# AdaLN block with linear attention and a mixture of experts: the first superblock in another order, LayerNorm and gates in pieces

## The reference, cut to what matters

```python
mod = (silu(c) @ wmod).reshape(1, 6, 1, -1)           # sa, ca, ga, sb, cb, gb
ga = sign(ga) * max(|ga|, 0.25); gb = likewise
h = layernorm(x) * (1 + ca) + sa                      # x: 1 x 4096 x 256
q, k, v = split(h @ w_qkv)                            # 16 heads of 64
q = softmax(q * SCALE, over the 64); k = softmax(k, over the tokens)
x = x + ga * ((per head q (k^T v)) @ w_out + b_out)
h = layernorm(x) * (1 + cb) + sb
x = x + gb * moe(h)                                   # 8 experts, top 2, gelu MLP 256-1024-256
```

## Time and profile before

| | us |
|---|---|
| median of 3 runs | 918.45 (918.38 to 919.68) |
| time of the profiled execution | 919.26 |
| its span | 917.5 |
| TensorE busy | 825.5 (90%) |
| VectorE busy | 571.7 (62%) |
| ScalarE busy | 498.4 (54%) |
| GpSimd busy | 344.2 (38%) |
| mean granted clock of TensorE | 0.95 |

### The profile page before, as it was taken

One profiled execution on the slowest core, in us unless ns is written; L12 is line 12 of the kernel. 1 busy time (PEld: TensorE's weight loads), 2 busy tenths in 40 slices (PEclk: granted clock), 3 DMA queues, 4 the chain that ended last, 5 costly groups with the idle time before them and its releaser, 6 DMA issues.

```text
span 917.5 us, 17514 instructions
## 1 busy us (share of the span) xinstructions
PE 825.5 (90%) x5836; PEld 770.2 (84%) x5837; DVE 571.7 (62%) x1257; ACT 498.4 (54%) x978; POOL 344.2 (38%) x304
## 2 busy tenths in 40 slices
PE   4849789999999888995499999999999999999994
PEld 4738678888888776984399999999999999999994
DVE  4677777777777652579546565656647575665552
ACT  4325446555554441359566665757567575665552
POOL 1213133334333131300135455455545555454442
PEclk9979899999999998995589999999999999999998
DMA  8300000000000013243515252252533525232222
GB/s 293 105 0 1 1 1 1 1 1 1 1 1 1 1 46 104 93 138 118 186 30 139 42 138 46 41 135 44 138 46 61 122 42 137 42 47 46 46 42 29
DMA packets 45214, 57.52 MB, mean 63 GB/s; under 512 B 7794, under 2 KB 39220, under 8 KB 45044
## 3 DMA queue, kind: packets, MB, share of 16 engines
q0 software_dynamic: 14400, 20.24, 13.7%
q1 hardware_dynamic: 30772, 36.76, 12.0%
HBM read 38.24 MB, written 18.75 MB: 62 GB/s over the span
## 4 chain that ended last, share of the span: by engine, by line
PE 79%; DVE 9%; issue 4%; ACT 4%; DMA 2%; POOL 1%; SPq 0%; ACTq 0%; DVEq 0%; POOLq 0%
PE ps L1436 23%; PE ps L1424 22%; PE ps L1269 8%; PE ps L1230 8%; PE ps L1288 6%; PE ps L1338 3%; PE ps L1278 2%; PE ps L1407 2%; ACT at_lo L736 2%; DVE q_max L857 1%; DMA wmod_sb<-in_L_wmod 1%; PE ps L1358 1%; DVE ln_s L841 1%; DVE k_blk L917 1%; PE ps L1348 1%
## 5 line engine op out<-in xcount | busy, mean ns | idle before, releaser
L791 ACT ACTIVATE hid<-ps,b_col 128x256 f32<-128x256 f32 x296 | 122.3, 464 | 120.9 <-PE ps L1424 120.9
L1151 DVE TENSOR_TENSOR hid_lo<-hid,hid_hi 128x512 fp32r<-128x512 f32 x148 | 102.5, 692 | 113.2 <-ACT hid_hi L799 111.1
L1436 PE MATMUL ps<-w_hi,hid_hi 128*128 128x256 f32 x592 | 170.2, 287 | 1.6 <-DVE hid_lo L1151 1.6
L1424 PE MATMUL ps<-xT_hi,w_hi 128*128 128x256 f32 x592 | 168.5, 285 | 2.2 <-DVE xT_lo L1128 2.2
L1424 PE MATMUL ps<-xT_hi,w_lo 128*128 128x256 f32 x592 | 168.3, 284 | 0.0
L1424 PE MATMUL ps<-xT_lo,w_hi 128*128 128x256 f32 x592 | 168.2, 284 | 0.0
L1436 PE MATMUL ps<-w_hi,hid_lo 128*128 128x256 f32 x592 | 166.5, 281 | 0.0
L1436 PE MATMUL ps<-w_lo,hid_hi 128*128 128x256 f32 x592 | 166.4, 281 | 0.0
L580 POOL DMA_INDIRECT out<-y,y_id x74 | 133.9, 1810 | 52.3 <-DVE y L1160 37.9
L504 POOL TENSOR_TENSOR q_n<-q_exp,q_rec 128x1024 f32<-128x1024 f32 x32 | 61.0, 1906 | 212.6 <-DVE q_rec L865 212.6
L1424 PEld LDWEIGHTS ps<-xT_hi,w_hi 128*128 128x128 f32 x592 | 113.8, 192 | 2.6 <-issue 2.6
(11 more groups left out here) (194 smaller groups left out, 1513.1 us busy)
## 6 DMA issues: line engine op xcount, KB each, us to landing
w_raw<-in_L_ffn_W SPq DMA_DIRECT2D x16, 1024.0 KB, 6.9
x_all<-in_L_attn_x SPq DMA_DIRECT2D x8, 512.0 KB, 10.3
out<-x_all SPq DMA_DIRECT2D x8, 512.0 KB, 3.0
xrows<-x_all SPq DMA_DIRECT2D x8, 512.0 KB, 3.0
wqk_raw<-in_L_attn_w_qkv SPq DMA_DIRECT2D x2, 1024.0 KB, 8.9
listed<-xrows,gid POOLq DMA_INDIRECT x76
out<-y,y_id POOLq DMA_INDIRECT x74
wmod_sb<-in_L_wmod SPq DMA_DIRECT2D x1, 1024.0 KB, 12.9
```

Source lines behind the costliest of these rows:

```text
L791: ins = act.activation(hid[:, m, :], ps[:, k, (m % 2) * BT:(m % 2 + 1) * BT], ACT.Gelu_apprx_tanh, bias=b1_col[:, bass.ds(e, 1), m])
L1151: dve.tensor_tensor(hid_lo[:, m, :], hid[:, m, :], hid_hi[:, m, :].bitcast(F32), ALU.subtract).then_inc(s_hid, 1)
L1424: last = pe.matmul(ps[:, k, (m % 2) * BT:(m % 2 + 1) * BT], w, a, start=st, stop=sp_)
L1436: last = pe.matmul(ps[:, Y0 + i, 0:D], a, w, start=m == 0 and st, stop=m == M - 1 and sp_)
```

## The change

Six things are moved or cut in another way; the arithmetic stays.

- The q columns of w_qkv are loaded and split in halves of 512 columns. The low parts of the k columns are computed by GpSimd (`w_low_k`), not by VectorE. GpSimd also clears ctx_acc.
- x of superblock 2 is loaded ahead of the k columns and of the second part of wmod.
- First superblock: ScalarE makes only the high part of h (`h_hi` returns), VectorE makes h_all and the low part (`h_0`). The first q product has its matmuls in the order in which their operands come. q(0,1) and q(0,2) stand before the second modulation, which ScalarE copies (`gate_raw`). The loop starts when only three q tiles have their maximum and two their sum; the rest of superblock 0's softmax is done in steps 0 and 1.
- LayerNorm is called for (0), (1, 2), (3, 4) and (5, 6, 7); the last two in pieces behind q_b in odd steps (`extra`).
- The gates are adjusted in steps 21 and 23; the router's weights are scaled in step 57 and centred while the context is folded.
- The gated bias is added by VectorE tile by tile in the last five superblocks: in odd steps from 25 on, in even steps from 40 on.

```diff
-            sp.dma_start(wqk_raw[:, :, 0:HD], wqk_t[:, :, 0:HD]).then_inc(s_wq, 16)
+            for i in range(2):
+                col = slice(i * 512, (i + 1) * 512)
+                sp.dma_start(wqk_raw[:, :, col], wqk_t[:, :, col]).then_inc(s_wq[i], 16)
+            for s in (1, 2):
+                sp.dma_start(x_all[:, s * ST:(s + 1) * ST, :], x_t[:, s * ST:(s + 1) * ST, :]).then_inc(s_x[s], 16)
             sp.dma_start(wqk_raw[:, :, HD:2 * HD], wqk_t[:, :, HD:2 * HD]).then_inc(s_wk, 16)
-            sp.dma_start(x_all[:, ST:2 * ST, :], x_t[:, ST:2 * ST, :]).then_inc(s_x[1], 16)
...
+            def w_low_k(c):
+
+                pool.wait_ge(s_whqk, 2 * C + c + 1)
+                pool.tensor_tensor(wqk_lo[:, c, HD:2 * HD], wqk_raw[:, c, HD:2 * HD], wqk_hi[:, c, HD:2 * HD].bitcast(F32), ALU.subtract).then_inc(s_wlk, 1)
...
-            def add_bias(s):
...
-                if s >= 1:
-                    add_bias(s - 1)
-            add_bias(SBN - 2)
-            add_bias(SBN - 1)
...
+            def h_0(c):
+
+                dve.wait_ge(s_hhi, c + 1)
+                link(dve.tensor_scalar(h_all[:, c, 0:STOK], ps[:, xt_bank(0, c), :], modc[:, 1, c:c + 1], modc[:, 0, c:c + 1], ALU.mult, ALU.add))
+                dve.tensor_tensor(h_q[:, 0, 1, c, :], h_all[:, c, 0:STOK], h_q[:, 0, 0, c, :].bitcast(F32), ALU.subtract).then_inc(s_hlo0, 1)
...
+            h_0(0)
+            h_0(1)
+            link(ln_stats(range(ST, 3 * ST)))
+            q_a(0, 0)
+            ln_finish((1, 2))
+            q_a(0, 1)
+            q_b(0, 0)
             dve.wait_ge(s_mod, 2)
+            dve.tensor_copy(modc[:, 2:4, :].rearrange("p k c -> p (k c)"), ps[:, MB, 0:2 * C]).then_inc(s_modc, 1)
+            q_a(0, 2)
+            q_b(0, 1)
...
+            def extra(n):
+
+                if n in (1, 3):
+                    t = 3 * ST + (n // 2) * ST
+                    link(ln_stats(range(t, t + ST)))
+                if n == 5:
+                    ln_var((3, 4))
+                    ln_root((3, 4))
+                if n == 7:
+                    ln_root((3, 4))
+                    ln_root((3, 4))
+                    ln_shift((3, 4))
+                if n in (9, 11, 13):
+                    t = 5 * ST + (n // 2 - 4) * ST
+                    link(ln_stats(range(t, t + ST)))
+                if n == 15:
+                    ln_var((5, 6, 7))
+                if n == 17:
+                    ln_root((5, 6, 7))
+                    ln_root((5, 6, 7))
+                if n == 19:
+                    ln_root((5, 6, 7))
+                    ln_shift((5, 6, 7))
+                if n == 21:
+                    gate_size()
+                if n == 23:
+                    gate_sign()
+                if n == 57:
+                    gate_mod()
...
+            def add_bias(t):
+
+                dve.wait_ge(s_gate, 1)
+                dve.wait_ge(s_xn, t // ST + 1)
+                dve.tensor_tensor(x_all[:, t, :], x_all[:, t, :], bo_bc[:, :], ALU.add).then_inc(s_bo, 1)
...
-                if s == 0 and j == 7:
-                    layer_norm((4, 5, 6, 7))
...
+                extra(n)
+                if j % 2 and s >= 3:
+                    add_bias((s - 3) * ST + j // 2)
+                if j % 2 == 0 and s >= 5:
+                    add_bias(s * ST + j // 2)
```

More of the change, by code:

```diff
@@ L236, in adaln_block @@
         s_c = sem("s_c")
-        s_wq = sem("s_wq")
+        s_wq = [sem(f"s_wq{i}") for i in range(2)]
         s_wk = sem("s_wk")
@@ L655, in _, with w_high @@
             act.activation(silu_t[:, :], silu_c[:, :], ACT.Exp, scale=-1.0).then_inc(s_silu_e, 1)
+            def w_high(half, c):
+                col = slice(half * 512, (half + 1) * 512)
+                act.activation(wqk_hi[:, c, col], wqk_raw[:, c, col], ACT.Copy).then_inc(s_whqk, 1)
+            act.wait_ge(s_wq[0], 16)
+            w_high(0, 0)
+            w_high(0, 1)
             norm_x(0)
-            act.wait_ge(s_wq, 16)
-            for c in range(C):
-                act.activation(wqk_hi[:, c, 0:HD], wqk_raw[:, c, 0:HD], ACT.Copy).then_inc(s_whqk, 1)
+            act.wait_ge(s_wq[1], 16)
+            w_high(1, 0)
+            w_high(1, 1)
             act.wait_ge(s_modr, 1)
@@ L687, in _ @@
                         q_e(s + 1, j // 2 - 1)
-                    elif not j and s:
+                    elif not j:
                         q_e(s, ST - 1)
@@ L896, in _ @@
[L896 to L899, removed]
-            dve.tensor_tensor(wg_mod[:, :, :], wg_raw[:, :, :], bc(modc[:, 3, :], 2, [P, C, E]), ALU.mult).then_inc(s_wgm, 1)
-            dve.wait_ge(s_bgp, 1)
-            dve.tensor_tensor(bg_bc[:, :], bg_bc[:, :], ps[:, MB, 0:E], ALU.add)
-            dve.wait_ge(s_wgm, 1)
-            dve.tensor_tensor(wg_mod[:, :, :], wg_mod[:, :, :], bc(ps[:, MB, E:2 * E], 1, [P, C, E]), ALU.subtract).then_inc(s_bgr, 1)
@@ L911, in _, with gate_mod, gate_size @@
-            q_b(0, 3)
+            dve.wait_ge(s_const, CONSTS)
+            def gate_mod():
+                dve.wait_ge(s_modc, 1)
+                link(dve.tensor_scalar(modc[:, 3, :], modc[:, 3, :], 1.0, None, ALU.add))
+                dve.tensor_copy(shift_b[:, :, :], bc(modc[:, 2, :], 2, [P, C, P]))
+                dve.wait_ge(s_small, 48)
+                dve.tensor_tensor(wg_mod[:, :, :], wg_raw[:, :, :], bc(modc[:, 3, :], 2, [P, C, E]), ALU.mult).then_inc(s_wgm, 1)
+            def gate_size():
+                dve.wait_ge(s_modg, 1)
+                dve.tensor_scalar(gate_s[:, :, :], gate_raw[:, :, :], 0.0, 2.0, ALU.is_ge, ALU.mult)
+                link(dve.tensor_scalar(gate_m[:, :, :], gate_raw[:, :, :], -1.0, None, ALU.mult))
+                link(dve.tensor_tensor(gate_m[:, :, :], gate_m[:, :, :], gate_raw[:, :, :], ALU.max))
@@ new lines, in gate_sign @@
+            def gate_sign():
+                link(dve.tensor_scalar(gate_m[:, :, :], gate_m[:, :, :], 0.25, None, ALU.max))
+                link(dve.scalar_tensor_tensor(gates[:, :, :], gate_s[:, :, :], 1.0, gate_m[:, :, :], ALU.subtract, ALU.mult))
+                dve.wait_ge(s_small, 48)
+                dve.tensor_tensor(bo_bc[:, :], bo_bc[:, :], gates[:, 0, :], ALU.mult).then_inc(s_gate, 1)
+            def extra(n):
[26 more added lines that the diff above has]
+                    gate_mod()
@@ L1238, in _ @@
             x_T(0)
+            steps = [(half, 0, c, low) for half in range(2) for c in range(C) for low in range(2)] + \
+                    [(half, 1, c, 0) for half in range(2) for c in range(C)]
+            for half, h_low, c, w_low in steps:
+                if h_low:
+                    pe.wait_ge(s_hlo0, c + 1)
+                else:
+                    pe.wait_ge(s_hhi, c + 1)
+                    pe.wait_ge(s_wlqk, half * C + c + 1)
+                w = (wqk_hi, wqk_lo)[w_low]
+                last = pe.matmul(ps[:, half, :], h_q[:, 0, h_low, c, 0:P], w[:, c, half * 512:(half + 1) * 512],
+                                 start=(h_low, c, w_low) == (0, 0, 0), stop=(h_low, c) == (1, C - 1))
+            last.then_inc(s_q, 1)
+            q_mm(0, 1)
+            q_mm(0, 2)
             pe.wait_ge(s_wmod[1], 16)
+            pe.wait_ge(s_modr, 1)
             modulation(MB, (3, 4))
@@ L1314, in _ @@
             c_mm(KN - 1)
+            pe.wait_ge(s_kev, KN)
+            pe.wait_ge(s_wgm, 1)
+            for c in range(C):
+                pe.matmul(ps[:, MW, 0:E], shift_b[:, c, :], wg_raw[:, c, :], start=c == 0, stop=c == C - 1)
+            pe.wait_ge(s_const, 4)
+            for c in range(C):
+                last = pe.matmul(ps[:, MW, E:2 * E], mean_w[:, :], wg_mod[:, c, :], start=c == 0, stop=c == C - 1)
+            last.then_inc(s_bgp, 1)
             pe.wait_ge(s_wvTc, 2)
```

132 lines of the change are left out of this document (66 added, 66 removed).

## The result

The changed kernel takes 893.45 us (median; 893.24 to 893.66), the kernel before 918.41 beside it: ratio 0.9719, 95% interval 0.9703 to 0.9735. The forecast was 891.0. The profiled execution took 893.38, its span is 891.7 against 917.5, so 25.8 us are to be found in it.

A forecast was written before the change was run, and what follows sets the result against it. TensorE held 79% of the chain of waits. 919.26 - 21.4 - 9.3 - 3.1 - 4.9 - 1.3 + 12.0 + 0.3 = 891.6 for a profiled execution, median 891; 886 to 896 at 0.57, wider range 879 to 904.

The forecast's parts named there:

- Start, 21.4: Start: VectorE's reordered queue brings the fifth k_blk at 52.3 instead of 73.76, gain 21.4 us, ends 16.2 and 23.6.
- Rival B: Start gives less, 16 instead of 21, or another wait of its kind loses up to 9: 896 to 901; chance 0.18.
- LayerNorm out of step 7, 9.3: LayerNorm of superblocks 4 to 7 leaves step 7: gain 9.3 us, 7.5 of wait and 1.8 of half clock.
- bias off GpSimd, 4.9: Steps 18, 26, 34, 42 and 50: k_new no longer waits for GpSimd's bias, 0.97 us each, gain 4.9.
- Pieces, 12.0: Odd-step chains behind q_rec, held until q_n ends, cost 12.0 us; X is the context sum's start after q_rec's start.
- rival A: Pieces in odd steps: the small chains are not held by q_n, total 879; chance 0.13.
- step 19's 3.1: Step 19: two h_lo follow q_n without a gap, one operation passes at each end; X 4.9, wait 3.1 us.
- Bias on VectorE, 0.3: 32 additions of 128x256 on VectorE are free except in step 44 behind h_lo, cost 0.3 us.
- Rival C: Odd steps: the bias loses the race to q_n, 0.85 us in each of 20 steps, total 908; chance 0.06.
- Last superblock, +1.3: Last superblock: k_new's holds go, part returns through the gate weights' scaling in step 57; gain 1.3 us (0 to 2.9).
- Rival D: Waits of 1 to 3 us in every second step from 15 to 23 drop TensorE to 1.2 GHz; 950; chance 0.04.
- Rival E: Start: the new order does nothing, as DMA or another late tile sets it, total 913; chance 0.02.

The follow-up runs named there:

- the one-piece kernel: Changed kernel with LayerNorm 5 to 7 finished wholly in step 17 and the gated bias made wholly in step 23: 895.53 us, ratio 0.9732.
- the third buffer: Changed kernel with the first superblock's third query tile's exponentials in a third buffer, the context's accumulator, cleared afterwards: 889.33 us, ratio 0.9674.
- its own undoing: Changed kernel with the gated bias back on GpSimd, four tiles at once behind the fourth q_norm, from step 26 on: 900.51 us, ratio 0.9796.
- pieces first: Changed kernel with the LayerNorm and gate pieces ahead of q_b in odd steps instead of behind it: 884.90 us, ratio 0.9629.
- The loop's part alone: Kernel before with its start kept; LayerNorm of superblocks 4 to 7 and gates in pieces, bias on VectorE: 912.20 us, ratio 0.9912.

## Why the prediction held, point by point

- **Start, 21.4**: 19.04 in the profile, inside 16.2 to 23.6. The list of VectorE's queue was right to 1.3 us up to 30 us (q_rec forecast to end at 29.2, at 30.5 in the trace; second modulation to 30, ended 30.1). It failed at "modc, q_a(0,2), q_b(0,1) 30 to 34.1": q_a(0,2) waited 2.07 for q_n(0,0), the release of one of two buffers, and the first k_blk, which the list allows at 35.2 when TensorE's k product ends, came at 36.39; the first k_new then ended at 38.47 instead of 37. The rest, 0.9, is TensorE's clock from 44.7 to 48 us. The wait of 2.09 in the trace of the kernel before should have been the warning. With the third buffer and a full clock the fifth k_blk stands at 51.81, where 52.3 was forecast. Rival B named this case; its 5 us or more did not come.
- **LayerNorm out of step 7, 9.3; gates out of step 15, 3.1; bias off GpSimd, 4.9**: shown by stretches two to four; step 15 without a piece lasts 4.11 in the one-piece kernel, where it lasted 7.17, and the bias is shown by its own undoing.
- **Pieces, 12.0**: the mechanism was right (rival A fell: operations of 12 elements were held for 1.2 to 1.8 us in every piece, and moved ahead of q_b they were not). The size was off: the waits X - 1.81 are 1.49, 1.19, 0.91, 1.12, 1.64, 1.53 and 1.40, sum 9.3, and pieces first gave back 7.8. The term that failed is step 19's 3.1: two operations passed before q_n began, one was held by it and one by the h_lo behind it (1.77 and 1.21 us), so X was 3.45 and not 4.9 (1.5 of the 2.7 too much); and that step has x^T of the next superblock on TensorE, so that it lasted 5.75 where the undisturbed one lasts 4.97.
- **The rule cited** (the Trainium skill, SBUF — State Buffer, Who interferes with whom), that two SBUF inputs or a two-port mode exclude GpSimd and one SBUF input otherwise doesn't: the trace agrees in both directions. scalar_tensor_tensor with two SBUF inputs took 1.76 and 2.27 us beside q_n, so the forecast's "7.3 if only the two shown forms held" is out; statistics, aggregates, the reductions k_blk and q_max and the sum with one input in PSUM kept their length beside q_n.
- **Bias on VectorE, 0.3**: step 44 lasted 4.75 instead of 4.43, 0.32. Rival C, that it loses the race to q_n, fell by 0.16 us. The odd steps 27, 35 and 43 last 4.98 or 4.99, over the 4.2 named as a sign of being wrong; they have x^T of the next superblocks, and lasted 5.04 and 5.07 before.
- **Last superblock, +1.3**: measured -1.25, the wrong sign. No trace shows a gain: at the clock of 0.91 that the kernel before had there the changed kernel's code takes 18.44 to 18.92 against 18.16. The forecast counted k_new's holds and not three new things: the bias addition of step 56 stands ahead of the sum for which TensorE waits (0.33 later, idle 2.73), with the clock at 0.50 behind it; and the scaling in step 57 came behind a memset of 0.91 and was held by q_n for 1.01. That these make the difference is argued from the trace; the edit that moves them gave 1.1 to 1.5 us within the intervals.
- **Rival D**, the clock falling for every second step: not in steps 15 to 23 here, but the one-piece kernel shows it twice, so the forecast's "passed at 1.00" from one execution of one wait was weak evidence. The sign "granted clock 1.00 from 30 to 340 us" did not hold: 0.63 from 44 to 48 us, 0.50 from 288 to 292.
- **Rival E** fell: the loop's part alone takes 912.2.

The profiled execution took 893.4 where the sum said 891.6: the shortfalls of the start and of the last superblock (2.4 and 2.6) were largely set off by the 3.2 too much for the stretch of the five pieces. That the total came within 1.8 us is in part luck; its two large terms, start and LayerNorm, were right by their mechanism.

## What to carry to other kernels

Price a small VectorE operation by what GpSimd is doing at its moment, and move it ahead of the instruction that starts GpSimd rather than cut it in pieces behind it: here 8 us for moving one line, where moving 1.3 us of VectorE's work into its idle time gave nothing. In a queue written by hand follow each release of a double buffer to the engine that gives it, in the first tiles too (2.07 and 2.09 us here). Where waits of 2 to 3 us end, expect the clock to differ from execution to execution, and do not credit an edit with 1.5 us that the same code gains and loses by itself.

## What the runs showed of the hardware

- A VectorE operation of 128x1 to 128x12 elements with two SBUF inputs, or a scalar addition on 8 or 12 elements in SBUF, took 0.16 or 0.17 us alone. Beside GpSimd's q_n it took 0.9 to 1.8, the less the later it came, and ended within 0.05 us of q_n's end. h_0(1)'s subtraction (0.69 us), which had begun at 17.68 before GpSimd's weight split of 18.13, kept its length.
- Two GpSimd instructions without a gap let one VectorE operation through between them: in step 19 the third operation of the root took 1.77 us up to q_n's end, the next 1.21 beside h_lo.
- After TensorE idle times of 2.73 and 2.89 us the granted clock was 0.72 over the next 6 us, after 2.88 and 3.25 us in two other kernels 1.00. The same idle time of 2.0 us at the same place of the same code gave 0.63 over 44 to 48 us in the changed kernel and 1.00 in three others. What decides between them was not found.
- Starts of the same instructions scatter by 1 us (first k_blk at 57.49 and 58.64 with the old start, 35.47 to 36.49 in six kernels with the changed one), and four steps of the last superblock by 2 us (18.44 to 20.36), the latter with a granted clock of 0.91 or of 0.82 to 0.83.
